# Diagonals of two attention layers moved to ScalarE, stacks moved to VectorE, and one layer's scattered transfers spread over more steps

## The reference

```python
x = x + _L0_attn_ref(xn, ...) + _L0_ffn_ref(xn, ...)      # feature-map attention, ternary weights
xn = _layernorm(x, axis=-1)
x = x + _L1_attn_ref(xn, ...) + _L1_ffn_ref(xn, ...)      # 16 heads of 64; 8 experts, best 2 of them
xn = _layernorm(x, axis=-1)
x = x + _L2_attn_ref(xn, ...) + _L2_ffn_ref(xn, ...)      # 16 heads of 8, causal; 8 experts, best 1
xn = _layernorm(x, axis=-1)
x = x + _L3_attn_ref(xn, ...) + _L3_ffn_ref(xn, ...)      # 16 heads of 8 + rope, causal; best 2 of 8 + shared
```

```python
logits = jnp.einsum('bhsd,bhtd->bhst', q, k) * scale
logits = jnp.where(mask, logits, neg_inf)
probs = jax.nn.softmax(logits, axis=-1)
out = jnp.einsum('bhst,bhtd->bhsd', probs, v)
```

## Time and profile before

| what | value |
| --- | --- |
| median of 3 runs | 2607.01 us |
| the profiled execution's own time | 2598.39 us |
| its span | 2596.6 us |
| attention of layer 1 (first exps of chunk 0 to first of chunk 1, of two chunks) | 274.6 to 390.5, to 462.3 us |
| a later chunk of layer 1 | 69.3 us (749.2 to 818.5) |
| a chunk of layer 2's attention | 47.6 us (1372.1 to 1419.7) |
| a chunk of layer 3's attention | 68.4 us (1979.5 to 2047.9) |
| mean granted TensorE clock | 0.883 |

### The profile page before, as it was taken

The page is one execution under the profiler, slowest core; times in us unless marked ns, Lnnn a source line. Parts: engine busy times, 40 slices in busy tenths (PEclk is TensorE's granted clock), DMA queues, the critical chain, the costliest instruction groups (busy, mean ns, idle before and its releaser), DMA issues.

```text
span 2596.6 us, 65873 instructions
## 1 busy us (share of the span) xinstructions
PE 2019.9 (78%) x23246; PEld 1394.1 (54%) x23247; DVE 1908.6 (74%) x4031; ACT 1377.8 (53%) x2794; POOL 723.5 (28%) x674
## 2 busy tenths in 40 slices
PE   1543679999999788815888887863899999998993
PEld 0213346666666566714555554543566666665662
DVE  2236667878788788866999998766677777776775
ACT  0231346767677655502766666430566666665552
POOL 0012685545455333323300000340720000000552
PEclk9775889999999999965988987885899998998997
DMA  8900012000000011220200000120100000000224
GB/s 226 168 0 0 26 37 72 2 3 3 3 2 2 10 48 49 61 73 15 85 2 2 2 2 5 48 64 12 51 18 2 2 2 2 2 2 10 63 62 124
DMA packets 109664, 88.07 MB, mean 34 GB/s; under 512 B 11240, under 2 KB 95816, under 8 KB 109424
## 3 DMA queue, kind: packets, MB, share of 16 engines
q1 hardware_dynamic: 97840, 60.82, 9.8%
q0 software_dynamic: 11584, 23.91, 2.7%
HBM read 45.26 MB, written 39.43 MB: 33 GB/s over the span
## 4 chain that ended last, share of the span: by engine, by line
PE 48%; DVE 28%; issue 12%; POOL 6%; ACT 3%; DMA 2%; DVEq 1%; SPq 1%; ACTq 0%; POOLq 0%
PE duo L1020 11%; PE mo L1020 10%; PE misc L1020 9%; PE acc L1020 6%; PE ob L1020 6%; DVE v L1969 4%; PE pt L1020 4%; DVE nmax L1958 3%; POOL slot_rows L623 2%; DVE nmax L2077 2%; DVE v L1802 2%; DVE nmax L1957 1%; DVE v L1794 1%; DVE region L2080 1%; DVE qT L1961 1%
## 5 line engine op out<-in xcount | busy, mean ns | idle before, releaser
L662 POOL DMA_INDIRECT results<-probT,dest_no x202 | 210.7, 1043 | 1158.5 <-ACT probT L701 1121.9
L637 POOL TENSOR_TENSOR v<-v 128x512 f16<-128x512 f32 x256 | 290.7, 1157 | 299.0 <-DVE region L2080 298.3
L1020 PE MATMUL ob<-wm,v 128*128 128x9 f16 (+1 forms) x5856 | 254.9, 180 | 72.8 <-DVE v L1969 48.9
L1020 PEld LDWEIGHTS ob<-wm,v 128*128 128x128 f16 x5856 | 222.6, 97 | 130.7 <-DVE v L1969 74.0
L903 ACT ACTIVATE v<-mo 128x384 f32<-128x384 f32 x352 | 174.2, 495 | 166.8 <-PE mo L1020 91.8
L961 ACT ACTIVATE v<-mo 128x512 f32<-128x512 f32 x256 | 153.4, 599 | 204.1 <-PE mo L1020 138.0
L1969 DVE TENSOR_TENSOR v<-v 128x768 f16<-128x768 f32 x256 | 243.5, 951 | 11.8 <-ACT v L904 11.8
L2077 DVE TENSOR_REDUCE nmax<-duo 128x2 f32<-128x512 f32 x256 | 164.8, 685 | 87.9 <-PE duo L1020 87.8
L1020 PE MATMUL duo<-kT,wm 128*128 128x256 f16 x1212 | 172.7, 279 | 55.0 <-DVE kT L1790 29.2
L1957 DVE TENSOR_REDUCE nmax<-duo 128x2 f32<-128x256 f32 x256 | 107.7, 421 | 133.6 <-PE duo L1020 132.8
L1020 PE MATMUL mo<-qT,kT 64*128 64x256 f16 (+1 forms) x2240 | 202.3, 274 | 0.0
(11 more groups left out here) (277 smaller groups left out, 4642.8 us busy)
## 6 DMA issues: line engine op xcount, KB each, us to landing
prob<-slot_rows SPq DMA_DIRECT2D x101, 130.0 KB
qT<-results SPq DMA_DIRECT2D x40, 256.0 KB, 3.1
slot_rows<-prob SPq DMA_DIRECT2D x4, 1300.0 KB, 18.6
slot_rows<-prob SPq DMA_DIRECT2D x4, 1235.0 KB, 20.1
xd<-in_L_ffn_w_dram SPq DMA_DIRECT2D x2, 2048.0 KB, 12.4
results<-probT,dest_no POOLq DMA_INDIRECT x202
slot_rows<-xd,slot_no POOLq DMA_INDIRECT x160, 2.3
x<-in_L_attn_x_dram SPq DMA_DIRECT2D x8, 256.0 KB, 4.6
```

Of the source, the lines that this page charges most:

```text
L637: pool.tensor_tensor(p16[:, p % 2, h, 1, :], p32[:, h, :], p16[:, p % 2, h, 0, :], ALU.subtract)\
L662: pool.indirect_dma_start(out=results[layer], out_offset=bass.IndirectOffsetOnAxis(ap=dest_no[:, 2 * b + t:2 * b + t + 1], axis=0), in_=y_ ...
L1020: return pe.matmul(dst, lhsT, rhs, start=start, stop=stop)
```

## The change

It has three parts.

1. In layers 2 and 3 the diagonal is no longer one VectorE instruction of 128 x 512 (identity times 1/16 times maxima). ScalarE makes it as four copies of 128 x 128 of a new constant `small_ident` (the identity divided by 16), each scaled by one column of `nmax`, in a new function `diagonals(i, p)`. ScalarE does that for step p+2 right after `exps(p)`, ahead of the gelu, of `keep_o` and of the preparation.
2. In layers 2 and 3 the 8 stacks of a chunk are copied by VectorE and no longer by ScalarE.
3. In layer 1 GpSimd issues one row transfer after each step, over chunks 0 to 3, and no longer four after each step of chunk 0. Its loop over chunks is written out.

```diff
@@ gpsimd, attention
-                per_step = TOP[layer] * ALL // STEPS
...
-                def chunk(i, parity, more):
+                if layer > 1:
+                    for n in range(TOP[layer] * ALL):
+                        send_row_tile(layer, n // ALL, n % ALL)
+                    return
+                for i in range(NCH):
                     for p in range(STEPS):
-                        if p + 1 < STEPS or more:
-                            at_step(diag_made, pool, stage, i, p + 1)
+                        if p + 1 < STEPS or i < NCH - 1:
+                            step1(diag_made, pool, i, p + 1)
                         prob_low(i, p, 0)
                         prob_low(i, p, 1)
-                        if isinstance(i, int) and i == 0:
-                            for n in range(per_step * p, per_step * p + per_step):
-                                send_row_tile(layer, n // ALL, n % ALL)
...
+                        n = i * STEPS + p
+                        if n < TOP[1] * ALL:
+                            send_row_tile(1, n // ALL, n % ALL)
@@ scalar, attention
-                def stack(i, n):
...
+                def diagonals(i, p):
+
+                    nmax_made.wait(act, stage, i, p)
+                    for n in range(4):
+                        ins = act.activation(diag2[:, p % 2, n // 2, n % 2, :], small_ident[:, :], ACT.Copy,
+                                             scale=nmax4[:, p % 2, n:n + 1])
+                    ins.then_inc(diag_made.sem, 1)
...
                         exps(i, p)
-                        for n in SELECT_AT.get(p, ()):
-                            stack(i, n)
+                        if p + 2 < STEPS:
+                            diagonals(i, p + 2)
+                        elif more:
+                            diagonals(i + 1, p + 2 - STEPS)
@@ vector, attention
                     dve.tensor_reduce(nmax4[:, p % 2, 2:4], duo[:, :, P:LINE], AX.X, ALU.max, negate=True)\
                         .then_inc(nmax_made.sem, 1)
-                    nmax_made.wait(dve, stage, i, p)
-                    dve.scalar_tensor_tensor(
-                        out=diag2[:, p % 2, :, :, :].rearrange("p q h c -> p (q h) c"),
...
+                def stack(i, n):
+
+                    g, kind = n // 2, n % 2
+                    sel_full.wait(dve, stage, i, n)
+                    dve.tensor_copy((k_stack if kind else q_stack)[:, g, :], (acc if n in (0, 2) else misc)[:, :])\
+                        .then_inc(stacked.sem, 1)
...
                             scale_o(i - 1, 3)
+                        for n in SELECT_AT.get(p, ()):
+                            stack(i, n)
                         if p == 2 and begun:
                             add(acc_full, x_made, i - 1, 0)
@@ vector, before the router of layer 1
+            dve.tensor_scalar(small_ident[:, :], ident[:, :], 1.0 / 16, None, ALU.mult).then_inc(v_ones, 1)
```

More of the change, by code:

```diff
@@ L239, in build_program @@
         r16 = sb("r16", [P, 2, 8])
+        small_ident = sb("small_ident", [P, P])
         oT = sb("oT", [P, 2, CHUNK])
@@ L856, in attention @@
                 stage = f"A{layer}"
-                def stack(i, n):
-                    g, kind = n // 2, n % 2
-                    sel_full.wait(act, stage, i, n)
-                    copy((k_stack if kind else q_stack)[:, g, :], (acc if n in (0, 2) else misc)[:, :]).then_inc(stacked.sem, 1)
+                def diagonals(i, p):
[4 more added lines that the diff above has]
+                    ins.then_inc(diag_made.sem, 1)
                 def high(i, n, at, src, scale):
@@ L879, in prepare @@
                         if p == 12:
-                            stack(i, 0)
                             keep_values(i, parity, 2)
-                        if p == 13:
-                            stack(i, 1)
                     else:
@@ L932, in attention @@
                     prepare(0, 0, p)
+                diagonals(0, 0)
+                diagonals(0, 1)
                 chunks1(act, chunk)
@@ L1427, in w1_block @@
                 return lambda hl: w1[:, hl, offset + j * P:offset + (j + 1) * P]
-            pe.wait_ge(v_ones, 3)
+            pe.wait_ge(v_ones, 4)
             def turn_x1(i):
@@ L1937, in prepare @@
                         if p == 12:
+                            stack(i, 0)
                             keep_values(i, parity)
+                        if p == 13:
+                            stack(i, 1)
                     else:
@@ L1959, in maxima @@
                         .then_inc(nmax_made.sem, 1)
-                    nmax_made.wait(dve, stage, i, p)
-                    dve.scalar_tensor_tensor(
-                        out=diag2[:, p % 2, :, :, :].rearrange("p q h c -> p (q h) c"),
-                        in0=ident[:, :].rearrange("p (o c) -> p o c", o=1).broadcast_to([P, 4, P]), scalar=1.0 / 16,
-                        in1=nmax4[:, p % 2, :].rearrange("p (a o) -> p a o", o=1).broadcast_to([P, 4, P]),
-                        op0=ALU.mult, op1=ALU.mult).then_inc(diag_made.sem, 1)
                 def pair_low(i, p):
```

## The result

The changed kernel takes 2619.86 us (median of 9 runs, 2616.47 to 2629.91), the kernel before 2605.44 beside it (9 runs, 2600.14 to 2608.66). The ratio is 1.0066, with a 95% interval of 1.0050 to 1.0082. The forecast was 2578 us, between 2542 and 2602: wrong in sign, and outside the range.

What follows compares the result with a forecast made beforehand. It took GpSimd to bound layer 1's chunk 0 and TensorE its later chunks, VectorE layer 2 and TensorE layer 3. Terms of -48, -2 and +21 us took 2607 to 2578 us, range 2542 to 2602.

Steps and rivals of the forecast that it cites:

- Spread, -48: Layer 1: row transfers, one a step, fit GpSimd's idle time; chunks 0 and 1 fall from 187.7 to 138.6 us.
- Price of a copy, 0.27 and four in 1.07: ScalarE, layers 2 and 3: a 128-column copy with a pointer operand takes 0.27 us, a diagonal's four 1.07.
- The loop, steps 0 to 10 of layer 2 in 29.7: Layer 2: ScalarE and VectorE wait for each other, 4.67 us per two steps plus extras; 29.7 us against 29.6 before.
- Steps 10 to 16 of layer 2 in 17.6: End of a layer 2 chunk: 6.1 us of ScalarE's work, then 6.4 and 5.1; 17.6 against 18.0 before.
- Steps 0 to 8 of layer 3 in 37.6: Layer 3: four loops of 8.10 us with a gelu, plus extras and `keep_o`; 37.6 us against 33.0 before.
- It had 1.34 to spare, the rest, 3.2, delays TensorE: Layer 3: ScalarE, 4.6 us later at step 8, absorbs 1.34 at step 9; net +2.6 a chunk, +21 us.
- `small_ident` below 1 us: The new constant for the scaled copies costs one instruction, below 1 us in all.
- The sum: Whole kernel: -48 in layer 1, -2 in layer 2, +21 in layer 3 make -29 us, from 2607 to 2578.
- (c): Rival: ScalarE's copies don't overlap, 0.37 us each, 1.5 a diagonal; slower, 2619 us; chance 0.08.
- (a): Rival: ScalarE really has the room in layers 2 and 3, TensorE stays layer 3's bound; 2526 us; chance 0.18.
- (b): Rival: layer 1's spread transfers don't hide and push `prob_low` into VectorE's diagonal; 2610 us, no change; chance 0.08.

Runs made afterwards that it cites:

- the fourth set: Three follow-up kernels run beside the kernel before on one chip; among them the kernel before with only layer 1's row transfers spread: 2551.97 us, 0.9791 of before.

## Why the prediction was wrong, step by step

- **Spread, -48:** right. Chunks 0 and 1 take 68.8 and 69.1 us, the stage 48.9 less; alone it is worth 2605.6 - 2552.0 = 53.6 us on the chip of the fourth set. VectorE's diagonal in layer 1 (L2087 after) takes 694 ns at most, where it took up to 3453.
- **Price of a copy, 0.27 and four in 1.07:** nearly right. Four start to start take 1.18 us (1375.46 to 1376.64 in ScalarE's timeline), 0.295 each. By the Trainium skill's figures (ScalarE: Activation LUTs, What ACT_TABLE_LOAD costs) I had estimated 0.29. Five groups at 0.11 more are 0.55, enough for the 0.4 between 29.7 and the 30.1 measured in layer 2's steps 0 to 10.
- **The loop, steps 0 to 10 of layer 2 in 29.7:** right. They take 30.1 at full clock, with the needless products, and 30.6 on average in the changed kernel.
- **Steps 10 to 16 of layer 2 in 17.6:** this failed. They take 21.1 on average. At full clock, with the needless products, they take 9.9 + 9.3 = 19.2, so 1.9 of the 3.5 is TensorE at its lower clock and 1.6 is a loop counted too short. Nearly all of the 1.6 is in steps 12 to 16 (12.9 against 11.5), for which the sum had `scale_o` and two stacks but not the preparation of the next chunk. In step 12 with the products VectorE is busy 3.58 of 3.61 us and TensorE for all of it. The 18.0 of before was that of one chunk, too; on average it is 19.1. The prediction priced every matmul at the clock that it had before, and took the 0.90 of layer 2 as given. The projections of p = 11 come out mostly at 1.2 GHz instead. Shown by the needless products: 15 of 18 us come back with more work on TensorE. Why the new loop makes the clock fall more often is only argued (two engines in series, so that TensorE waits a little in most steps). In the kernel before TensorE idles for 0.6 to 0.9 us in steps 4 to 6 of a chunk as well.
- **Steps 0 to 8 of layer 3 in 37.6:** right at 38.2 in two of chunks 1 to 6, but 39.8 to 42.9 in the four others, 40.3 on average. The two have a granted clock of 1.00, the others 0.96 to 0.88, and the longest have the lowest: 2.1 us on average go with the lower clock. In the chunk of 42.2 and in chunk 1 step 3 is alike (6.7 us, 1.1 of it idle on TensorE), but step 4 runs at full clock in chunk 1 and at the lower level in the other:

```profile
1912.04:1914.74 2.70, 2.70 (x28) 2.19 (x27) 1.07 (x2) 2.70 (x9) 0.00 (x0) 1.00 0.00 0
2057.81:2063.36 5.55, 5.55 (x31) 4.35 (x30) 2.08 (x5) 2.79 (x9) 0.00 (x0) 0.50 0.00 0
```

- **"It had 1.34 to spare, the rest, 3.2, delays TensorE":** this failed. The loss at step 8 is 5.2 in the best chunks (38.2 against 33.0) and 7.0 on average, and steps 8 to 13 take 21.2 us before and after on average: nothing is absorbed. TensorE waited inside the stretch, where the gelu first gives 20 us back, rather than at its end, so the spare time at step 9 was no cushion. Given back at the chunk's end were 1.2, not 0.6. Net 5.7 a chunk against 2.6: of the 3.1 between, 2.4 are the loss of steps 0 to 8 above the 4.6 forecast and 1.3 the cushion, less the 0.6 more given back.
- **`small_ident` below 1 us:** failed, 5.3 us in M1. I counted its instruction (0.16 us) and not its 512 bytes a partition.
- **The sum:** -29 against +14 to +21. Of the 50 us between, layer 3 has 19, layer 2 has 21, M1 and gaps some 10.
- **Rivals:** (c) named 2619, but its mechanism (0.37 a copy) is refuted at 0.295; it hit the time by chance. (a), that ScalarE has the room, is refuted by 6.06 busy of 6.12 us and 2.66 of 2.66 in a pair of steps of layer 3 (2072.97 to 2081.75 in the changed kernel). VectorE's relief is worth something all the same, at the end of layer 3's chunks: steps 13 to 16 take 14.4 us before, 13.1 in the changed kernel and 10.4 with the diagonals on GpSimd. (b), transfers that don't hide, is refuted by layer 1.

Still open: what decides when TensorE's clock falls, in layer 3 above all, where the needless products didn't stop it (step 4 of one chunk still fell to 0.50), and what in the buffer's place slows `place`.

## What to carry to other kernels

Room in an engine's busy share is not room in its queue. Before moving an operation, ask what it waits for and what stands behind it: here copies that wait for late maxima blocked the exponentials and the gelu, while the same job on an engine with nothing behind it (GpSimd, which takes 1.2 times as long as the four copies) gained 27 us in layer 3. Put a price on TensorE's clock as well: where a change may add short waits in each step, work out the heaviest piece behind them at the lower level too.

## What the hardware showed that I had not expected

- More work made layer 2 faster: 128 x 3 needless products of 256 columns, 15 us less (354.3 to 339.1 on seven chunks), with their mean granted clock at 1.00 against 0.78.
- A burst of 32 or 64 indirect transfers at a stage's start costs nothing on the chips where before takes 2605 (first step 3 to 4 us) and 16 to 49 us on the two where it takes 2708 (first step 19.1 to 52.5 us). Spread one a step it is 3.6 to 3.7 on those two as well, though only in kernels that also make the diagonals on GpSimd. The spread alone differs by 112.5 us in span between one chip of each kind (2657.2 and 2544.7), and the first chunks of layers 2 and 3 have 83 of them. That is most of why GpSimd's version is at 0.937 there and at 0.967 to 0.973 elsewhere. What the engines wait for in those steps the profile doesn't name: in the spread alone ScalarE stands idle for 8.2 and 9.2 us there, and no engine of the core releases it.
- The price of two engines side by side differs by layer: `pair_low` takes 951 to 954 ns without GpSimd's product, 993 with it in layer 3, and 1256 in layer 2 (1363 with the needless products too). The product itself takes 1438 ns in layer 2 and 1542 in layer 3 of the kernel that has both there; GpSimd's 128 x 512 subtraction in layer 1 takes 1154.
